# Two row sums and one copy move from ScalarE to VectorE in the last stage of a transformer layer

## What is computed

```python
def _layernorm(x, axis=-1, eps=1e-5):
    m = jnp.mean(x, axis=axis, keepdims=True)
    v = jnp.var(x, axis=axis, keepdims=True)
    return (x - m) / jnp.sqrt(v + eps)

def _L0_ffn_ref(x, ternary_weight, bias, act_scale):
    scale = jnp.maximum(act_scale, 1e-05)
    x_int = jnp.clip(jnp.round(x / scale), -QB, QB)
    x_dq = jnp.nan_to_num(x_int * scale, nan=0.0, posinf=10000.0, neginf=-10000.0)
    w = ternary_weight.astype(jnp.float32) - 1.0
    return jnp.einsum('bsi,oi->bso', x_dq, w) + bias

x = _layernorm(x + _L0_attn_ref(x, L0_attn_W_qkv, L0_attn_W_o), axis=-1)
x = _layernorm(x + _L0_ffn_ref(x, L0_ffn_ternary_weight, L0_ffn_bias, L0_ffn_act_scale), axis=-1)
```

## Time and profile before

| | us |
|---|---|
| timed runs, median of 2 | 1761.1 (1760.19 to 1762.0) |
| profiled execution, device time | 1757.4 |
| its span on the slowest core (core 4) | 1755.8 |
| spans of the other cores | 1732.8 to 1753.5 |
| core 4, busy | PE 1149.2, ACT 1007.4, DVE 562.5, POOL 30.6 |

### The profile page before, as it was taken

One profiled execution on the slowest core, in us unless ns is written; L12 is line 12 of the kernel. 1 busy time (PEld: TensorE's weight loads), 2 busy tenths in 40 slices (PEclk: granted clock), 3 DMA queues, 4 the chain that ended last, 5 costly groups with the idle time before them and its releaser, 6 DMA issues.

```text
span 1755.8 us, 18405 instructions; the slowest of 8 cores (1732.8 to 1755.8 us)
## 1 busy us (share of the span) xinstructions
PE 1149.2 (65%) x5064; PEld 379.1 (22%) x5064; DVE 562.5 (32%) x1145; ACT 1007.4 (57%) x1227; POOL 30.6 (2%) x55
## 2 busy tenths in 40 slices
PE   1001788888876626677777878788888885565664
PEld 0001333333332201111111211121112211222221
DVE  0002222222223315533332223222221123666664
ACT  0002344444444427688888888888888984454543
POOL 0001000000000000000000000000000000000000
PEclk9999999999999958799899999999989997787877
DMA  9994654555443162322233132422322001111211
GB/s 101 119 172 101 110 117 106 112 121 121 117 96 77 42 119 75 99 82 78 79 114 114 58 114 68 140 75 75 128 98 75 1 1 48 48 62 59 72 49 48
DMA packets 112818, 153.30 MB, mean 87 GB/s; under 512 B 38736, under 2 KB 93008, under 8 KB 108368
## 3 DMA queue, kind: packets, MB, share of 16 engines
q1 hardware_dynamic: 65536, 113.26, 20.5%
q0 software_dynamic: 13648, 30.48, 12.3%
q10 hardware_dynamic: 33536, 8.39, 2.7%
HBM read 132.26 MB, written 46.14 MB: 102 GB/s over the span
## 4 chain that ended last, share of the span: by engine, by line
PE 37%; ACT 24%; DVE 12%; issue 11%; DMA 10%; another core or an unknown queue 4%; ACTq 2%; DVEq 0%; SPq 0%; POOL 0%; POOLq 0%
ACT exp_b L484 17%; PE pAV L506 8%; PE pC L364 6%; DVE exp_b L495 5%; PE pSC L469 5%; PE pR L612 5%; PE pR L699 3%; PE pA L312 3%; PE pB L312 3%; ACT kraw L318 3%; DMA w_kvT<-wqkv_bf 2%; DMA q_scr<-krot 2%; ACT recb L515 2%; DMA maskb<-masks 2%
## 5 line engine op out<-in xcount | busy, mean ns | idle before, releaser
L484 ACT ACTIVATE exp_b<-pSC 128x1024 bf16<-128x1024 f32 x640 | 606.9, 1048 | 147.9 <-PE pSC L474 123.3
L506 PE MATMUL pAV<-exp_b,v_run 128*128 128x512 bf16 x1280 | 417.3, 411 | 94.3 <-DVE exp_b L495 93.3
L495 DVE TENSOR_TENSOR exp_b<-exp_b,maskb 128x512 bf16<-128x512 bf16 x512 | 211.5, 425 | 371.1 <-ACT exp_b L484 310.2
L469 PE MATMUL pSC<-q_run,k_run 64*128 64x512 bf16 x640 | 253.8, 405 | 116.6 <-ACT exp_b L484 102.4
L474 PE MATMUL pSC<-q_run,k_run 64*128 64x512 bf16 x640 | 258.6, 413 | 0.0
L469 PEld LDWEIGHTS pSC<-q_run,k_run 64*128 64x128 bf16 x640 | 57.6, 94 | 415.1 <-issue 415.1
L506 PEld LDWEIGHTS pAV<-exp_b,v_run 128*128 128x128 bf16 x1280 | 77.4, 98 | 277.8 <-issue 277.8
L364 PE MATMUL pC<-w_kvT,x_T 128*128 128x512 bf16 x512 | 115.7, 379 | 0.0
L267 PE MATMUL pD<-identb,w_st 128*128 128x128 bf16 x32 | 4.0, 306 | 137.5 <-DVE w_st L261 137.5
L690 PE MATMUL pT<-identb,xq_bf 128*128 128x128 bf16 x128 | 16.2, 306 | 117.0 <-DVE mst L634 110.1
L612 PE MATMUL pR<-w_oT,attn_n 128*128 128x512 bf16 x256 | 85.5, 508 | 7.1 <-issue 7.1
(11 more groups left out here) (103 smaller groups left out, 975.7 us busy)
## 6 DMA issues: line engine op xcount, KB each, us to landing
v_scr<-v_stg SPq DMA_DIRECT2D x32, 512.0 KB, 3.4
v_run<-v_scr SPq DMA_DIRECT2D x8, 2048.0 KB, 9.4
v_run<-v_scr SPq DMA_DIRECT2D x8, 1536.0 KB, 7.9
x_tm<-x_kv POOLq DMA_DIRECT2D x8, 1024.0 KB, 11.2
k_scr<-krot SPq DMA_DIRECT2D x64, 128.0 KB, 2.6
v_run<-v_scr SPq DMA_DIRECT2D x8, 1024.0 KB, 5.5
k_run<-k_scr SPq DMA_DIRECT2D x8, 1024.0 KB, 5.6
xo<-x_own SPq DMA_DIRECT2D x16, 512.0 KB, 4.4
```

The lines of the kernel that those rows point to most:

```text
L469: s.add("T", (lambda sb_, bi, t: lambda te: te.matmul(pSC[sb_][:, 0:512], k_run[bi][0:64, t * 128:(t + 1) * 128], q_run[bi][0:64, :], star ...
L484: s.add("SC", (lambda eb, sb_: lambda sc: sc.activation(exp_b[eb][:, :], pSC[sb_][:, :], ACTF.Exp))(eb, sb_), reads=[f"pSC{sb_}"], writes= ...
L495: s.add("V", (lambda eb, moff, half: lambda v: v.tensor_tensor(exp_b[eb][:, half * 512:(half + 1) * 512], exp_b[eb][:, half * 512:(half + ...
L506: s.add("T", (lambda eb, bi, t, hh, n, pit: lambda te: te.matmul(pAV[pit][:, hh * 512:(hh + 1) * 512], v_run[bi][:, t * 256 + hh * 128: t ...
```

## The change

Both Identity passes of ACT (st 2 and st 11) go. In their place DVE computes the plain row sum of y1f with `reduce_sum` into a free column of mst (+1 and +9). A new 128x1 DVE instruction at the head of st 3 and st 12 multiplies it by 1/D into the column that the Identity pass used to write (+2 and +10). In st 8 the copy of pT to xq_T is a DVE `tensor_copy` in place of an ACT `copy`. The Square passes stay on ACT. Since a sum and the Square pass behind it write under the same mst name, the Square pass waits for the sum. The helper `ln_stats` is not called and not changed. The three other parts of the diff are these; those for st 11 and st 12 repeat st 2 and st 3 with columns +9 to +11:

```diff
                 elif st == 2:
-                    s.add("SC", (lambda bi, moff: lambda sc: sc.activation(
-                        sqb[bi % 2][:], y1f[bi][:], ACTF.Identity, scale=1.0 / D,
-                        accum_out=mst[:, moff + 2:moff + 3]))(bi, moff),
-                        reads=[f"y1f{bi}"], writes=["sqb", f"mst{bi}"])
+                    s.add("V", (lambda bi, moff: lambda v: v.reduce_sum(
+                        mst[:, moff + 1:moff + 2], y1f[bi][:], axis=AX))(bi, moff),
+                        reads=[f"y1f{bi}"], writes=[f"mst{bi}"])
                     s.add("SC", (lambda bi, moff: lambda sc: sc.activation(
                         sqb[bi % 2][:], y1f[bi][:], ACTF.Square, scale=1.0 / float(np.sqrt(D)),
                         accum_out=mst[:, moff + 3:moff + 4]))(bi, moff),
                         reads=[f"y1f{bi}"], writes=["sqb", f"mst{bi}"])
                 elif st == 3:
+                    s.add("V", (lambda bi, moff: lambda v: v.tensor_scalar(
+                        mst[:, moff + 2:moff + 3], mst[:, moff + 1:moff + 2], 1.0 / D, None,
+                        op0=ALU.mult))(bi, moff),
+                        reads=[f"mst{bi}"], writes=[f"mst{bi}"])
...
                             reads=[f"xq_bf{bi}", "identb"], writes=["pT"])
-                    s.add("SC", (lambda bi: lambda sc: sc.copy(xq_T[bi][:], pT[:, :]))(bi),
+                    s.add("V", (lambda bi: lambda v: v.tensor_copy(xq_T[bi][:], pT[:, :]))(bi),
                           reads=["pT"], writes=[f"xq_T{bi}"])
```

More of the change, by code:

```diff
@@ L717, in emit_stage @@
                 elif st == 11:
[L718 to L721, removed]
+                    s.add("V", (lambda bi, moff: lambda v: v.reduce_sum(
+                        mst[:, moff + 9:moff + 10], y1f[bi][:], axis=AX))(bi, moff),
+                        reads=[f"y1f{bi}"], writes=[f"mst{bi}"])
                     s.add("SC", (lambda bi, moff: lambda sc: sc.activation(
@@ L726, in emit_stage @@
                 elif st == 12:
+                    s.add("V", (lambda bi, moff: lambda v: v.tensor_scalar(
+                        mst[:, moff + 10:moff + 11], mst[:, moff + 9:moff + 10], 1.0 / D, None,
+                        op0=ALU.mult))(bi, moff),
+                        reads=[f"mst{bi}"], writes=[f"mst{bi}"])
                     s.add("V", (lambda bi, moff: lambda v: v.scalar_tensor_tensor(
```

## The result

| | before | changed |
|---|---|---|
| median of all runs, us | 1762.5 (10 runs) | 1791.9 (11 runs) |
| ratio to before | 1 | 1.0179, 95% interval 1.0149 to 1.0210 |
| profiled execution, us | 1757.4 | 1788.5 |
| its span, slowest core, us | 1755.8 | 1787.0 |

The changed kernel is 1.8% slower, about 31.5 us. The ratio, and with it the 31.5 us, compares the means of the 7 and 9 executions in which the chip was in its faster state, while the medians in the table count all. Up to the last stage nothing differs (its first L612 starts at 1459.90 us before and at 1460.13 now). The page's slices show that stage, the last seven or so, with a lower granted clock, 6 to 7 tenths where the earlier trace rows had mostly 7 to 8.

What follows compares the result with a forecast made beforehand. Bound: a circle of waits between TensorE and VectorE in the last stage. Sums 31.9, ends 1.7 and clock 2.8 make 36.4 us; 1757.4 became 1793.8, plus 3.7 for timed runs 1797.5, called 1798, range 1787 to 1808.

Steps and rivals of the forecast that it cites:

- The circle and the place of the sums: Last stage: TensorE and VectorE wait for each other in turn, 17.07 us per block; both sums stand between L713 and L671.
- The price of a sum: Each row sum on VectorE costs 1.14 us of queue; two in each of 14 blocks, 31.9 us.
- the dearer of the two bounds: A sum's queue cost lay between 0.61 us (single-source instructions) and 1.14 us (two-source); the forecast took 1.14.
- The copy, ScalarE, the scalings within the blocks: Blocks 2 to 15: xq_T copy on VectorE, ScalarE's lost passes and the 1/D scalings change nothing, 0 us.
- The ends: Outside blocks 2 to 15: block 16's sum 1.14, block 1 0.1, first and last tiles 0.8, copies -0.3 us.
- The clock: TensorE's half-clock time per block in blocks 2 to 15, mean 4.9 instead of 4.5 us: +2.8 us.
- the exposed copy: Blocks 16 and 17, where L612 is absent: xq_T copy 0.32 us shorter on VectorE, -0.3 us for both.
- the slow stretch: Time from a block's transposes during which TensorE runs at half clock; expected to wander between 3.4 and 5.9 us.
- The rival of a late clock: Blocks settle at a late clock rise, 5.9 us or more at half clock in each: 1804.5 us, chance 0.20.

Runs made afterwards that it cites:

- e4: Changed kernel with the st 2 sum emitted right behind L621 and the st 11 sum with its Square pass behind st 7: 1.0032 times the kernel before.
- e2: Kernel before with only the copy of xq_T moved from ScalarE to VectorE: 1.0001 times the kernel before.
- e9: Changed kernel with row sums as accumulators of L621 and L713 instead of reductions, and st 10 emitted behind st 7: 0.9714 times the kernel before.
- e5: Changed kernel with one more useless VectorE multiply on a 128x768 scratch tile behind the st 11 sum: 1.0261 times the kernel before.
- e3: Changed kernel with only the st 2 sum moved, emitted with st 1 right behind L621: 1.0125 times the kernel before.

## Why the prediction was right, and where it was off

The forecast was 1798 us, within 1787 to 1808, and 1792 was measured. The likeliest class is not borne out: I gave 0.62 to slower by over 2%, and the ratio is 1.0179, its interval reaching from 1.0149 to just beyond 2%. The forecast stood less than 2 us above that line, so this hung on its smaller terms, the clock's above all.

- *The circle and the place of the sums*: as read. The order L716, L625, L721, L674 is the one forecast, and moving the sums off it (e4) takes the cost away with the work unchanged.
- *The price of a sum*: 1.14 us of queue forecast, 1.13 measured, 1.21 us recorded. The duration is that of the two-source rows, the dearer of the two bounds. By the Trainium skill (VectorE: DVE Perf Modes, the perf-mode tier table) a tensor_reduce has no faster mode; the trace agrees, with 1.21 us beside the 1.21 us of L674's two-source form. 14 blocks: 31.9 forecast, 14 x 2.26 = 31.6 measured.
- *The copy, ScalarE, the scalings within the blocks*: nothing forecast, nothing found (e2; L716 still waits 1.72 us). That ScalarE's relief is worth nothing held for this order of emission alone: with st 10 behind st 7 the traces give it some 0.7 us per block (e9).
- *The ends*: 1.14 + 0.1 + 0.8 - 0.3 = 1.7 us forecast. The way from tile 0's L612 to the transposes of block 2 grew from 22.09 to 22.36 us (+0.3). Between the transposes of blocks 16 and 17 it went from 16.01 to 15.68 us (-0.3, although a sum was added: the clock rose earlier in that block, where L702 took 4.92 us and L699 had taken 6.28; six of the other cores have 16.4 us there). From there to the last L751 (L757 now) it grew from 13.39 to 14.27 us (+0.9). That is 0.8 us in all. The -0.3 us that I gave to the exposed copy is not shown by any run; e2 has none.
- *The clock*: this is the mis-sized term. I forecast +2.8 us for the 14 blocks, bounds -7.7 to +9.8. Measured on the slowest core: 30.1 - 31.6 = -1.5 us; cores whose 14 blocks took 271.9 us have -0.3 by the same account. Beside its own blocks before, each core has between -0.8 and +2.2 us, so the forecast's +2.8 was too much on every core. I had the slow stretch wander between 3.4 and 5.9 us, the values that the first blocks showed, with a mean of 4.9. It goes from 2.71 to 5.63, mean 4.33, a little below the 4.5 of before. The stretch of 2.71 is outside the range that I took for its bounds, and its block of 18.55 us is outside the 19.3 to 20.1 that I gave; in the kernel before the shortest block of any core was 16.67 us, so no row showed a stretch like it. Of "wander" only so much was right that it isn't the same in each block. That this term did little harm was luck: 4.9 was chosen between two bounds, and nothing in the working led to a cycle whose mean is 4.33.
- *The rival of a late clock* did not happen here. e5 shows that it is real: 0.47 us further along it does, at 5.68 us, near the 5.9 that I priced it by.

The sum is then 31.6 - 1.5 + 0.8 = 30.9 us, and the span grew by 31.2; the last stage of the slowest core also began 0.2 us later. Against the 36.4 us of the forecast, 4.3 of the 5.5 us too much are the clock's term, 0.9 the ends', 0.3 the sums'.

## What to carry to other kernels

Where no engine is full, look for the circle of waits and ask of each new instruction whether it stands on it: the same two reductions cost 31 us behind an instruction that waited for TensorE and about 4 us, at the last tiles, when emitted elsewhere (e4). Before adding a reduction over a tile, see whether the instruction that writes the tile can accumulate it. And an order that lets independent work pass a waiting instruction can be worth more than any of this (1.6% by itself, 2.9% with the accumulators), but each such order has to be read on every engine's queue.

## What the hardware showed that I had not expected

- A scalar_tensor_tensor on VectorE with an accumulator output takes no longer than without (1.28 us, and the next instruction still starts 1.20 us after it); its read of the accumulator is 0.08 us, ScalarE's is 0.19 us.
- A VectorE instruction that reads the result of the one just ahead of it starts 0.11 us after that one's recorded end, an independent one 0.08 us ahead of it: L721 starts 1.39 us after L716 in e3, L625 1.20 us in the changed kernel. The order of two instructions in the queue is worth 0.19 us here.
- In this stage the loop's length and the granted clock settled into a pattern with each other. With the circle's constant part at 15.0 us all blocks end up at 17.07 us with 4.29 us at half clock; at 17.2 us they go round three lengths, 18.55, 19.50 and 19.98 us, and at 17.7 us they settle on one length again, 20.48 us with 5.68 us at half. So 2.3 us more work gave 2.15 us per block, and the next 0.47 us gave 1.14 us. A small change of such a loop need not be worth what its instructions last.
